# Experts' token rows kept in 32-bit floats, turned two blocks ahead, and a router stage with logits from 16-bit halves

## The chip, the cores and the metric

One core of one Trainium2 chip runs the whole program. The metric is device time in microseconds (us); the median of three runs of the kernel before is 1145.98 us (1141.5 to 1146.59).

## What is computed

Input x is 8 x 256 tokens of width 512, with a context of the same shape. Two layers follow each other: a long convolution used as attention, a quantised feed-forward net, a cross attention, and a mixture of experts. The change is in the last of them. Cut to what matters:

```
x2  = layernorm(x)                                   # 2048 tokens, D = 512
aff = sigmoid(x2 @ wa)                               # 16 experts
p, i = top_k(aff, 2);  p = p / sum(p)
expert(e, x2) = (gelu(x2 @ g[e] + gb[e]) * (x2 @ w1[e] + b1[e])) @ w2[e] + b2[e]     # F = 256
routed = sum over the 2 chosen experts of p * expert(e, x2)
shared = expert of sg[0] + expert of sg[1], on all tokens
out = x + shared + routed        # x2 also enters as the layer's own input in the kernel: x + x2
```

Products are made to nearly 32-bit precision from 16-bit (bf16) halves: a number is split into a high half and the rest, and three of the four products of halves are summed (`three_products`, L1138).

## The kernel before

Partitions hold 128 tokens; NT = 16 such tiles make the 2048 tokens. Every stage is one block with a program for each engine (SyncE issues most DMAs, VectorE is DVE, ScalarE is ACT, GpSimd is POOL, TensorE is PE). The engines' orders are written out by hand; they wait for each other by counted semaphores. A stage begins when all engines have left the one before.

**Attention** (`stage_attention`, from L1565 on) comes ahead of the router. In its last microseconds DVE makes the first two normalised tiles of the router (`RouterScales`, L1537, tiles r_xn).

**Router stage** (`stage_router`, L2029 to L2182, from 728 to 776 us). For each tile t of 16:

- DVE normalises a tile into xn, one of two buffers (L1561).
- ACT makes the high half of the token-major row (r_rows, L2167), DVE the low half (L2110), and SyncE stores both as 1024 bf16 numbers a token to token_rows in DRAM (L2076). This is what the experts later gather.
- PE transposes the tile (four 128x128 float transposes, L2143, into one of four PSUM buffers ps_rx). ACT copies it once as floats (r_xT, L2171) and once as bf16 high half (L2174, tile s_xT), DVE makes the low half (L2112). Tiles 0 to 11 of the turned halves are stored too (L2079).
- PE computes the logits from the float copy: four float matmuls with 16 columns (L2149), into ps_rl.
- ACT writes the scaled residual (L2178); for ten tiles SyncE stores it to mid_rows (L2082).
- The six weights of the two shared experts (512 KB each) are loaded by SyncE at the stage's start (L2071), their high halves made by POOL (L2095) and their low halves by DVE (L2116, `weight_lows`).

At the end ACT takes the exponential of all logits (L2180), DVE finishes the sigmoid (L2130, L2131), and the stage ends.

**Route and shared stage** (`stage_route_and_shared`, 776 to 885 us): top 2, the table of slots that sorts (token, expert) pairs into NBLK = 47 blocks of 128, the shared experts, and the loading and splitting of all routed experts' up and gate weights into the SBUF tensor expert_weights. At its end POOL gathers the rows of the first two blocks (L2375).

**Experts stage** (`stage_experts`, L2609 to L2954, from 885 us on). Block n of 47 goes through these steps:

- POOL gathers 128 rows from token_rows into e_rows (an indirect DMA of 256 KB, L2664), two blocks ahead. After it POOL issues the scatter of an older block's results (L2669), in the order gather(n + 2), scatter(n - 2).
- PE turns the rows: eight bf16 transposes (L2871), four of the high and four of the low halves, into ps_ex. The row's columns are taken with a step of four (`c:...:DC`), since the weights' partitions are laid out so. Here the transposed data is the stationary operand, loaded by LDWEIGHTS, and the identity is the moving one.
- ACT copies the high (L2736), DVE the low half (L2781) to e_xT.
- DVE copies the block's expert from expert_weights to e_w (L2774).
- PE makes gate and up (24 matmuls each, e_w stationary, e_xT moving, ps_eg and ps_eu), ACT the gelu (L2729), DVE the product with up (L2787), ACT and DVE its halves (L2742, L2795), PE the down product (six matmuls of 512 columns, ps_ed) with e_parts, which SyncE loads per block (512 KB, L2686), ACT scales it by the routing weight (e_yo, L2720).

PE's order is up(n), turn(n + 1), down(n - 1). On ACT it is out_rows(n - 2), gelu(n), x_split(n + 1), y_split(n); on DVE gate(n), x_split(n + 1), y_split(n), weights(n + 2). From block 32 on SyncE also loads the residual tiles (16 of 256 KB, L2694) while the blocks run.

After the last block come two chunks of the shared experts that were kept back (late_up, late_down), and the sums.

The bf16 view with a step of two (`a.bitcast(BF16)[:, :, :, 1::2]`, L1588), by which the upper 16 bits of floats serve as high halves with no copy, is already used in attention, for the stationary operand of the values' matmuls (L1865, tiles at_pf and kw).

Of the kernel before, what the change touches and what calls it, by code (L numbers as in the profile page):

```python
# [15 lines left out]
P = 128  # L16
# [1514 lines left out]

FRONT = 4
# [4 lines left out]
class RouterScales:  # L1537


    def __init__(self, sb, semaphore):  # L1540
        self.mean, self.var, self.tmp, self.rstd, self.gain, self.shift = (
            sb(f"r_{n}", [P, NT], F32) for n in ("mean", "var", "tmp", "rstd", "gain", "shift"))
        self.xn = [sb(f"r_xn{i}", [P, D], F32) for i in range(2)]
        self.var_ready, self.rstd_ready, self.scaled, self.xn_ready = (
            semaphore(f"rs_{n}") for n in ("var", "rstd", "sca", "xn"))

# [13 lines left out]
    def normalise(self, dve, x, t):  # L1560
        dve.tensor_scalar(self.xn[t % 2][:, :], x[:, t, :], self.mean[:, t:t + 1], self.rstd[:, t:t + 1], ALU.subtract, ALU.mult)\  # L1561
# [3 lines left out]
def stage_attention(k, ks, last_keys, v_hi, v_lo, qw, ow, vectors, x_mean, x_rstd, stats, qs, kb, ahead, front):  # L1565
# [3 lines left out]
    with ExitStack() as ctx:  # L1569
# [59 lines left out]
        def _(sp):  # L1629
# [364 lines left out]
SH_N = 2  # L1994
FE = 256
# [10 lines left out]
SETS = 4  # L2006
# [22 lines left out]
def stage_router(k, stats, xaff, sgu, sd, down_bias, kept, front, x_places):  # L2029
# [4 lines left out]
    with ExitStack() as ctx:  # L2034
# [4 lines left out]
        xT = two("r_xT", [P, DC, P], F32)  # L2039
        rows = [sb(f"r_rows{i}", [P, 2, D], BF16) for i in range(SETS)]  # L2040
# [5 lines left out]
        raw = [sb(f"r_raw{i}", [P, 1024], F32) for i in range(6)]  # L2046
        w_loaded, w_high = [k.semaphore(f"r_w{i}") for i in range(6)], k.semaphore("r_whi")
        rows_high, rows_low = k.semaphore("r_rh"), k.semaphore("r_rl")
# [3 lines left out]
        wa_loaded, dve_step, added, x_psum, xT_ready, x_high, x_low, logits, exped = (  # L2052
            sem(n) for n in ("wa", "dve", "add", "xp", "xT", "xh", "xl", "log", "ex"))
# [8 lines left out]
        def _(sp):  # L2062
# [6 lines left out]
            for n in range(6):  # L2069
                src = k.ins[("L1_ffn_sg", "L1_ffn_sw1")[dst[n][2]] if n < 4 else "L1_ffn_sw2"][dst[n][1], :, :]  # L2070
                sp.dma_start(raw[n][:, :].rearrange("p (c n) -> p c n", c=D // P if n < 4 else F2),  # L2071
                             src.rearrange("(c p) n -> p c n", p=P)).then_inc(w_loaded[n], 16)
            for t in range(NT):
                q = t % SETS
                sp.wait_ge(rows_low, t + 1)
                sp.dma_start(rows_dram[t, :, :], rows[q][:, :, :].rearrange("p s d -> p (s d)")).then_inc(rows_stored[q], 16)  # L2076
# [12 lines left out]
        def _(pool):  # L2089
            pool.memset(bias_raw[:, :], 0.0).then_inc(bias_zeroed, 1)  # L2090
            pool.wait_ge(front.var_ready, 2)
            front.inverse_root(k, pool, LAST)
            for n in range(6):
                pool.wait_ge(w_loaded[n], 16)
# [4 lines left out]
        def _(dve):  # L2099
            link = Link(dve, dve_step)  # L2100

            def normalise(t):
                dve.wait_ge(x_psum, t - 1)
                dve.wait_ge(rows_low, t - 1)
                front.normalise(dve, k.x, t)

            def split(t):
                q = t % SETS
                dve.wait_ge(rows_high, t + 1)
                dve.tensor_tensor(rows[q][:, 1, :], xn[t % 2][:, :], rows[q][:, 0, :], ALU.subtract).then_inc(rows_low, 1)  # L2110
# [6 lines left out]

            for t in range(NT):
# [8 lines left out]
                if t >= 5 and t % 2:  # L2127
                    weight_lows((t - 5) // 2)
# [8 lines left out]
        def _(pe):  # L2137
            def turn(t):
# [3 lines left out]
                for c in range(DC):  # L2142
                    last = pe.transpose(psX[t % SETS][:, c * P:(c + 1) * P], xn[t % 2][:, c * P:(c + 1) * P], k.ident[:, :])  # L2143
                last.then_inc(x_psum, 1)

            def score(t):
                pe.wait_ge(xT_ready, t + 1)
                for c in range(DC):
                    last = pe.matmul(psL[:, t * E_N:(t + 1) * E_N], xT[t % 2][:, c, :], wa[:, c, :], start=(c == 0), stop=(c == DC - 1))  # L2149
                last.then_inc(logits, 1)  # L2150

            pe.wait_ge(wa_loaded, 16)
            turn(0)
            turn(1)
            for t in range(NT):
# [5 lines left out]
        def _(act):  # L2161
            for t in range(NT):
                q = t % SETS
                act.wait_ge(xn_ready, t + 1)
                if t >= SETS:
# [909 lines left out]
```

## Time and profile before

| what | value |
|---|---|
| median of three runs | 1145.98 us |
| the profiled execution's own time | 1146.08 us |
| its span (first to last instruction) | 1144.3 us |
| PE busy | 1044.4 us (91%) |
| DVE, ACT, POOL busy | 830.1, 685.7, 582.5 us |
| bytes moved by DMA | 194.61 MB, 170 GB/s in the mean |
| router stage | 728 to 776 us |
| experts stage with its late part | 885 us to the end |

In the views below, times are us and "mean ns of one" is in nanoseconds. PEld is the weight load of TensorE, which overlaps its matmuls. PEclk is the granted clock of TensorE as a share of 2.4 GHz, so 0.5 is the lower level of 1.2 GHz. Matmuls overlap in the pipeline: the distance of two of them, not the length of one, is what a stream of them costs.

### The profile page before, as it was taken

Reading aid. Unit: us, or ns where it says so; the run is one execution under the profiler, and the core shown is the slowest. Engines: PE = TensorE matmul, PEld = TensorE weight load, DVE = VectorE, ACT = ScalarE, POOL = GpSimd, SP = SyncE. Lnnn points to the kernel's source line nnn. Section 1 sums busy time; section 2 is a strip of 40 time slices with the busy share of each in tenths; the row PEclk is TensorE's granted clock in tenths of the full one; section 3 lists DMA queues with packets and bytes.
Section 4 is the critical chain, followed back from the end, with each engine's and each line's share of the span. In section 5 each row is a group of like instructions: output and inputs, shape, how many; then the busy total and the mean of one; then the engine's idle time right before and its main releaser. Section 6 shows DMA issues by size and latency. Waiting matters only on the chain. (4 is left out here: it accounts for less than half of the span.)

```text
span 1144.3 us, 24806 instructions
## 1 busy us (share of the span) xinstructions
PE 1044.4 (91%) x9247; PEld 782.7 (68%) x9247; DVE 830.1 (73%) x1468; ACT 685.7 (60%) x1203; POOL 582.5 (51%) x635
## 2 busy tenths in 40 slices
PE   5999998679997998858999999798898899999997
PEld 5777776634443776547888876596675788888884
DVE  5589999869998788756666676698766555555538
ACT  4574773679986646557877775395354354445431
POOL 5444445425445354448777787403785355555520
PEclk9999999779999999959999999658999899999998
DMA  8483431859886223222222220484786467678879
GB/s 317 161 261 120 163 124 38 158 166 230 232 224 181 85 73 104 70 86 57 57 57 57 58 56 2 149 317 169 204 276 222 166 235 247 227 250 279 304 256 363
DMA packets 133705, 194.61 MB, mean 170 GB/s; under 512 B 67990, under 2 KB 70204, under 8 KB 132792
## 3 DMA queue, kind: packets, MB, share of 16 engines
q1 hardware_dynamic: 117256, 149.45, 41.9%
q0 software_dynamic: 8544, 24.68, 6.8%
q10 hardware_dynamic: 7792, 18.96, 5.1%
q8 instruction: 72, 1.18, 0.4%
q14 instruction: 41, 0.34, 0.1%
HBM read 127.47 MB, written 44.48 MB: 150 GB/s over the span
## 5 line engine op out<-in xcount | busy, mean ns | idle before, releaser
L470 PE MATMUL ps_y<-kv,toep 128*128 128x288 f32 x640 | 158.2, 410 | 3.4 <-PEq L173 2.2
L470 PEld LDWEIGHTS ps_y<-kv,toep 128*128 128x128 f32 x640 | 122.0, 192 | 39.0 <-DMA toep<-taps_padded 3.2
L1790 DVE TENSOR_REDUCE at_negmax<-ps_s 128x4 f32<-128x1024 f32 x64 | 78.2, 1222 | 49.2 <-PE ps_s L1840 49.2
L164 POOL TENSOR_TENSOR kv<-kx 128x1024 f32<-128x1024 f32 x32 | 60.6, 1895 | 86.3 <-DVE outT L524 37.6
L2669 POOL DMA_INDIRECT expert_results<-e_yo,target x47 | 68.9, 1467 | 57.9 <-ACT e_yo L2720 57.9
L1141 PEld LDWEIGHTS ps_eg<-e_xT,e_w 128*128 128x128 bf16 x1128 | 69.0, 100 | 15.2 <-DVE e_w L2774 2.5
L1141 PE MATMUL ps_eg<-e_xT,e_w 128*128 128x128 bf16 x1128 | 73.1, 223 | 4.1 <-DVE e_xT L2781 4.0
L1141 PE MATMUL ps_eu<-e_xT,e_w 128*128 128x128 bf16 x1128 | 72.0, 221 | 0.0
L2774 DVE COPY e_w<-expert_weights 128x4096 bf16 x47 | 57.7, 1227 | 18.3 <-issue 18.3
L2664 POOL DMA_INDIRECT e_rows<-token_rows,token x45 | 43.7, 970 | 50.9 <-PE ps_ex L2871 45.0
L2787 DVE SCALAR_TENSOR_TENSOR e_y<-ps_eu,e_bias,e_y 128x128 f32<-128x128 f32 x94 | 28.6, 346 | 55.4 <-PE ps_eu L1141 53.5
L1094 PE MATMUL ps_fH<-w1T,f_qaT 128*128 128x512 bf16 x256 | 64.2, 395 | 3.4 <-PEq L636 2.1
L1141 PEld LDWEIGHTS ps_eu<-e_xT,e_w 128*128 128x128 bf16 x1128 | 66.4, 99 | 0.0
L1110 PE MATMUL ps_fY<-w2T,f_qbT 128*128 128x512 bf16 x256 | 57.7, 379 | 5.7 <-DMA f_qbT<-f_qb 5.7
L2736 ACT ACTIVATE e_xT<-ps_ex 128x512 bf16<-128x512 bf16 x47 | 28.1, 597 | 57.8 <-PE ps_ex L2871 57.8
L1687 POOL TENSOR_TENSOR vw<-kw 128x1024 bf16<-128x1024 f32 x32 | 60.6, 1895 | 3.1 <-ACT kw L1743 3.1
L1687 POOL TENSOR_TENSOR vw<-at_pf 128x1024 bf16<-128x1024 f32 x32 | 60.6, 1895 | 0.0
L494 DVE TENSOR_TENSOR prod<-ps_y,qx 128x1024 f32<-128x1024 f32 x32 | 39.1, 1222 | 24.8 <-ACT ps_y L417 24.8
L1141 PE MATMUL ps_ed<-e_parts,e_yhi 128*128 128x512 bf16 x188 | 55.9, 379 | 0.7 <-DVE e_ylo L2795 0.4
L1749 ACT ACTIVATE qs<-ps_m 32x256 bf16<-32x256 bf16 x128 | 48.1, 376 | 11.5 <-PE ps_m L1852 8.4
L2729 ACT ACTIVATE e_y<-ps_eg,e_bias 128x128 f32<-128x128 f32 x94 | 29.4, 364 | 39.4 <-PE ps_eg L1141 26.0
L1094 PEld LDWEIGHTS ps_fH<-w1T,f_qaT 128*128 128x128 bf16 x256 | 25.4, 100 | 36.5 <-issue 5.7
(450 smaller groups left out, 3075.2 us busy)
## 6 DMA issues: line engine op xcount, KB each, us to landing
e_parts<-down_parts SPq DMA_DIRECT2D x47, 512.0 KB
w_raw<-in_L_ffn_w ACTq DMA_DIRECT2D x32, 512.0 KB, 4.2
toep<-taps_padded SPq DMA_DIRECT2D x32, 256.0 KB, 3.6
f_draw<-in_L_ffn_rw SPq DMA_DIRECT2D x16, 512.0 KB, 4.3
down_parts<-f_dparts SPq DMA_DIRECT2D x16, 512.0 KB, 2.9
expert_weights<-expert_results SPq DMA_DIRECT2D x16, 512.0 KB, 10.0
x_res<-in_x SPq DMA_DIRECT2D x4, 1024.0 KB
c_in<-in_ctx SPq DMA_DIRECT2D x4, 1024.0 KB, 14.3
```

What stands on the lines that cost most here:

```text
L164: pool.tensor_tensor(pairs[:, :, :, 0:HD0], x[:, :, 0:HD0].unsqueeze(2).broadcast_to([P, ROWS_N, WIDE, HD0]), sliding_rows(x, 0, 1, WIDE), ...
L470: last = pe.matmul(y[:, l * B:(l + 1) * B, :, WIDE - 1:], toep[h % 2][:, (DC - 1 - l + m) * P:(DC - l + m) * P], kv[h % 2][:, m * B:(m + 1 ...
L494: dve.tensor_tensor(slots[:, :, 0:WIDE, :], blocks(y)[:, :, :, WIDE - 1:PITCH - 1], sliding_rows(q, 0, 1, WIDE), ALU.mult) .then_inc(prod_ ...
L1094: pe.matmul(psH[:, f, :].rearrange("p (a t) -> p a t", t=P), qaT[p][:, c, :], k.w1T[:, f * DC:(f + 1) * DC, c, :], start=(c == 0), stop=False)
L1110: last = pe.matmul(psY[p][:, :].rearrange("p (a t) -> p a t", t=P), qbT[p][:, c, :], k.w2T[:, :, c, :], start=(c == 0), stop=(c == FC - 1))
L1141: instruction = pe.matmul(out, stationary[a], moving[b], start=first and n == 0, stop=last and n == 2)
L1687: pool.tensor_tensor(pl[u % 4][:, :, :, :], pf[u % 4], ph[u % 4], ALU.subtract)\
L1749: act.activation(qs[nb % 2][STACK:, h0 + j, c, :], psM[rows, :, :].rearrange("p q t -> p (q t)"), ACT.Copy)\
L1790: dve.tensor_reduce(negmax[u % 2][:, :].rearrange("p (j q) -> p j q", j=2), psS[:, :, :, :], AX.X, ALU.max, negate=True).then_inc(max_read, 1)
L2664: pool.indirect_dma_start(out=rows[j % 2], out_offset=None, in_=k.scratch["rows"], in_offset=bass.IndirectOffsetOnAxis(ap=token[:, j:j + 1 ...
L2669: pool.indirect_dma_start(out=k.scratch["results"], out_offset=bass.IndirectOffsetOnAxis(ap=target[:, j:j + 1], axis=0), in_=yo[j % 2], in ...
L2774: dve.tensor_copy(w1[j % 2][:, :, :, :].rearrange("p h c f -> p (h c f)"), W[:, bass.ds(e, 1), :, :, :].rearrange("p o h c f -> p (o h c f ...
```

## The change

Four parts, as the diff has them.

1. token_rows holds one float row (512 floats, 2048 bytes, as many as before) instead of two bf16 halves. The router stores xn itself; r_rows and its two operations a tile go away. xn gets four buffers instead of two.
2. In the experts stage PE turns the float rows with four float transposes in place of eight bf16 ones. ACT copies them as floats to e_xf, whose upper 16 bits, seen with a step of two, are the high half; DVE subtracts to make the low half e_xlo. The turn, ACT's and DVE's part come two blocks ahead (PE: up(n), turn(n + 2), down(n - 1)), with the order on DVE gate(n), y_split(n), x_split(n + 2), weights(n + 2), and two turns ahead of the loop.
3. The logits are computed by `three_products` on the turned halves and on the halves of wa (12 bf16 matmuls a tile); the float copy r_xT goes away, and score(t) waits for x_low instead.
4. Two of the six shared weights are loaded at the start of attention; the other four are loaded at tiles 1, 3, 5 and 7 of the router stage. `weight_lows` begin at tile 3, and POOL makes the first weight's high half ahead of the inverse root.

```diff
 class RouterScales:
-        self.xn = [sb(f"r_xn{i}", [P, D], F32) for i in range(2)]
+        self.xn = [sb(f"r_xn{i}", [P, D], F32) for i in range(SETS)]
+        self.raw = [sb(f"r_rawa{i}", [P, D // P * FE], F32) for i in range(RAW_AHEAD)]
+    def load_shared_weight(self, sp, k, n):
+        sp.dma_start(self.raw[n][:, :].rearrange("p (c n) -> p c n", c=D // P), self.shared_weight(k, n)).then_inc(self.raw_loaded[n], 16)
...
 stage_attention, sync:
+            for n in range(RAW_AHEAD):
+                front.load_shared_weight(sp, k, n)
             for b, u in STEPS:
...
 stage_router, sync:
-            for n in range(6):
-                src = ...
-                sp.dma_start(raw[n]..., src...).then_inc(w_loaded[n], 16)
             for t in range(NT):
-                sp.wait_ge(rows_low, t + 1)
-                sp.dma_start(rows_dram[t, :, :], rows[q][:, :, :]...).then_inc(rows_stored[q], 16)
+                if t % 2 and RAW_AHEAD + t // 2 < 6:
+                    sp.dma_start(raw[n]..., front.shared_weight(k, n)).then_inc(w_loaded[n], 16)
+                sp.wait_ge(xn_ready, t + 1)
+                sp.dma_start(rows_dram[t, :, :], xn[q][:, :]).then_inc(rows_stored[q], 16)
 vector:
             def normalise(t):
-                dve.wait_ge(x_psum, t - 1)
-                dve.wait_ge(rows_low, t - 1)
+                if t >= SETS:
+                    dve.wait_ge(x_psum, t - SETS + 1)
+                    dve.wait_ge(rows_stored[t % SETS], 16 * (t // SETS))
             def split(t):
-                dve.wait_ge(rows_high, t + 1)
-                dve.tensor_tensor(rows[q][:, 1, :], xn[t % 2][:, :], rows[q][:, 0, :], ALU.subtract).then_inc(rows_low, 1)
-                if t >= 5 and t % 2:
-                    weight_lows((t - 5) // 2)
+                if t >= 3 and t % 2 and t < 15:
+                    weight_lows((t - 3) // 2)
 tensor:
             def score(t):
-                pe.wait_ge(xT_ready, t + 1)
+                pe.wait_ge(x_low, t + 1)
                 for c in range(DC):
-                    last = pe.matmul(psL[...], xT[t % 2][:, c, :], wa[:, c, :], ...)
+                    last = three_products(pe, psL[...], [turned[t % SETS][:, s, c, :] for s in range(2)],
+                                          [wa_parts[:, s, c, :] for s in range(2)], c == 0, c == DC - 1)
 scalar:
-                act.activation(rows[q][:, 0, :], xn[t % 2][:, :], ACT.Copy).then_inc(rows_high, 1)
-                act.activation(xT[t % 2][:, :, :], chunks(psX[q][:, :]), ACT.Copy).then_inc(xT_ready, 1)
...
 stage_experts:
-        xT = two("e_xT", [P, 2, DC, P], BF16)
+        xf = two("e_xf", [P, DC, P], F32)
+        x_hi = [a.bitcast(BF16)[:, :, 1::2] for a in xf]
+        x_lo = two("e_xlo", [P, DC, P], BF16)
 scalar:
-                act.activation(xT[j % 2][:, 0, :, :], psX[0][:, :, :], ACT.Copy).then_inc(x_high, 1)
+                act.activation(xf[j % 2][:, :, :], psX[j % 2][:, :, :], ACT.Copy).then_inc(x_high, 1)
-                if n + 1 < NBLK:
-                    x_split(n + 1)
+                if n + 2 < NBLK:
+                    x_split(n + 2)
 vector:
-                dve.tensor_copy(xT[j % 2][:, 1, :, :], psX[1][:, :, :]).then_inc(x_low, 1)
+                dve.tensor_tensor(x_lo[j % 2][:, :, :], psX[j % 2][:, :, :], x_hi[j % 2], ALU.subtract).then_inc(x_low, 1)
 tensor:
             def turn(j):
                 pe.wait_ge(rows_loaded[j % 2], 16 * (j // 2 + 1))
-                for h in range(2):
-                    for c in range(DC):
-                        last = pe.transpose(psX[h][:, c, :], rows[j % 2][:, h * D + c:(h + 1) * D:DC], k.ident_b[:, :])
+                if j >= 2:
+                    pe.wait_ge(x_low, j - 1)
+                for c in range(DC):
+                    last = pe.transpose(psX[j % 2][:, c, :], rows[j % 2][:, c:D:DC], k.ident[:, :])
             for n in range(NBLK + 1):
-                if n + 1 < NBLK:
-                    turn(n + 1)
+                if n + 2 < NBLK:
+                    turn(n + 2)
```

## Rows read from the trace of the kernel before

**Rows 1.** Experts stage, windows: busy time (x count) of each engine, clock, DMA.

```profile
900.00:1045.00 145.00, 144.98 (x2031) 121.40 (x2028) 84.72 (x165) 72.61 (x163) 80.78 (x65) 1.00 0.69 238
1045.00:1094.00 49.00, 48.64 (x683) 40.72 (x681) 28.30 (x56) 23.80 (x55) 25.84 (x21) 1.00 0.89 307
```

**Rows 2.** The chain that ended last, one block: start, length, what.

```profile
1087.13 0.45 PE ps_ex L2871 x8
1087.58 1.29 PE ps_ed L1141 x6
...
1091.55 0.45 PE ps_ex L2871 x8
```

**Rows 3.** Router stage, window: its full stretch, columns as in Rows 1.

```profile
732.00:764.00 32.00, 30.80 (x147) 29.87 (x146) 28.80 (x52) 28.71 (x52) 8.07 (x7) 0.50 1.03 377
```

**Rows 4.** Router stage, timeline: start, length, engine, line, op.

```profile
756.08 1.09 PE L2143 MATMUL ps_rx<-ident,r_xn 128*128 128x128 f32 x4
756.97 1.73 PE L2149 MATMUL ps_rl<-r_wa,r_xT 128*128 128x16 f32 x8
758.54 1.09 PE L2143 MATMUL ps_rx<-ident,r_xn 128*128 128x128 f32 x4
...
772.71 0.38 ACT L2180 ACTIVATE r_exp<-ps_rl 128x256 f32<-128x256 f32 x1 [1.44 <-PE ps_rl L2149]
```

**Rows 5.** Start of the experts stage, PE alone, timeline.

```profile
896.39 2.72 PE L1141 MATMUL ps_eg<-e_xT,e_w 128*128 128x128 bf16 x24 [1.66 <-DVE e_xT L2781]
900.57 0.61 PE L2871 MATMUL ps_ex<-ident_b,e_rows 128*128 128x128 bf16 x8
```

**Rows 6.** Groups of DVE instructions by line, 728 to 773 us.

```profile
L2112 DVE TENSOR_TENSOR s_xT<-ps_rx,s_xT 128x512 bf16<-128x512 f32 x16 | 11.0, 684 | 5.1 <-ACT s_xT L2174 5.1
L1561 DVE TENSOR_SCALAR r_xn<-x_res,r_mean,r_rstd 128x512 f32<-128x512 f32 x14 | 7.9, 565 | 0.0
L2116 DVE TENSOR_TENSOR sgu<-r_raw,sgu 128x1024 bf16<-128x1024 f32 x4 | 4.9, 1217 | 0.0
```

**Rows 7.** Attention, a run of float transposes of adjacent columns, timeline.

```profile
606.74 1.07 PE L1929 MATMUL ps_p<-ident,at_o 128*128 128x128 f32 x8
```

**Rows 8.** Float transposes of every second column (8 bytes apart), timeline.

```profile
872.18 0.44 PE L2588 MATMUL ps_stab<-ident,s_table 47*128 47x47 f32 x2
```

**Rows 9.** Float transposes and weight loads by tile: ns min/median/max of one, first and last start.

```profile
L1929 PE MATMUL ps_p<-ident,at_o x64: 272/273/474, 550.7 to 718.0; 128*128 128x128 f32 x64
L1929 PEld LDWEIGHTS ps_p<-ident,at_o x64: 138/141/230, 550.7 to 717.8; 128*128 128x128 f32 x64
L2588 PE MATMUL ps_stab<-ident,s_table x2: 292/304/317, 872.2 to 872.3; 47*128 47x47 f32 x2
L2588 PEld LDWEIGHTS ps_stab<-ident,s_table x2: 194/205/216, 872.2 to 872.3; 47*128 47x128 f32 x2
L1865 PEld LDWEIGHTS ps_o<-v_hi,at_pf x256: 96/97/151, 506.4 to 712.2; 128*128 128x128 bf16 x128
L2871 PEld LDWEIGHTS ps_ex<-ident_b,e_rows x376: 111/113/131, 885.1 to 1096.1; 128*128 128x128 bf16 x188
```

**Rows 10.** Experts stage, one block on POOL, timeline.

```profile
965.38 1.50 POOL L2669 DMA_INDIRECT expert_results<-e_yo,target  x1 [1.05 <-ACT e_yo L2720]
966.89 0.61 PE L2871 MATMUL ps_ex<-ident_b,e_rows 128*128 128x128 bf16 x8
967.77 0.97 POOL L2664 DMA_INDIRECT e_rows<-token_rows,token  x1 [0.90 <-PE ps_ex L2871]
```

**Rows 11.** Early experts stage: a gather's issue, and windows in which it lands.

```profile
891.14 0.97 POOL L2664 DMA_INDIRECT e_rows<-token_rows,token  x1 [5.90 <-issue]
...
892.00:894.00 2.00, 2.00 (x22) 1.90 (x19) 0.00 (x0) 0.00 (x0) 0.11 (x1) 0.81 0.47 135
```

**Rows 12.** A scatter of the loaded stretch, and ACT waiting for it.

```profile
1058.41 1.55 POOL L2669 DMA_INDIRECT expert_results<-e_yo,target  x1 [1.05 <-ACT e_yo L2720]
...
1067.50 0.69 ACT L2720 ACTIVATE e_yo<-ps_ed,weight 128x512 f32<-128x512 f32 x1 [1.61 <-DMA expert_results<-e_yo,target]
```

More of the change, by code:

```diff
@@ L1993 @@
 E_N = 16
-SH_N = 2
-FE = 256
 F2 = FE // P
@@ L2038, in stage_router @@
         gain, shift, xn, scaled, xn_ready = front.gain, front.shift, front.xn, front.scaled, front.xn_ready
-        xT = two("r_xT", [P, DC, P], F32)
-        rows = [sb(f"r_rows{i}", [P, 2, D], BF16) for i in range(SETS)]
+        wa_parts = sb("r_wap", [P, 2, DC, E_N], BF16)
         turned = [kept[q // ST][:, q % ST, :, :].rearrange("p s (c t) -> p s c t", c=DC) for q in range(SETS)]
@@ L2142, in turn @@
                 for c in range(DC):
-                    last = pe.transpose(psX[t % SETS][:, c * P:(c + 1) * P], xn[t % 2][:, c * P:(c + 1) * P], k.ident[:, :])
+                    last = pe.transpose(psX[t % SETS][:, c * P:(c + 1) * P], xn[t % SETS][:, c * P:(c + 1) * P], k.ident[:, :])
                 last.then_inc(x_psum, 1)
             def score(t):
-                pe.wait_ge(xT_ready, t + 1)
+                pe.wait_ge(x_low, t + 1)
                 for c in range(DC):
-                    last = pe.matmul(psL[:, t * E_N:(t + 1) * E_N], xT[t % 2][:, c, :], wa[:, c, :], start=(c == 0), stop=(c == DC - 1))
+                    last = three_products(pe, psL[:, t * E_N:(t + 1) * E_N], [turned[t % SETS][:, s, c, :] for s in range(2)],
+                                          [wa_parts[:, s, c, :] for s in range(2)], c == 0, c == DC - 1)
                 last.then_inc(logits, 1)
-            pe.wait_ge(wa_loaded, 16)
             turn(0)
             turn(1)
+            pe.wait_ge(wa_low, 1)
             for t in range(NT):
@@ L2624, in stage_experts @@
         bias = sb("e_bias", [P, 2 * F2, NBLK], F32)
-        psX = [ctx.enter_context(nc.psum_tensor(f"ps_ex{i}", [P, DC, P], BF16)) for i in range(2)]
+        psX = [ctx.enter_context(nc.psum_tensor(f"ps_ex{i}", [P, DC, P], F32)) for i in range(2)]
         late_psG, late_psU = ([ctx.enter_context(nc.psum_tensor(f"ps_e{n}{i}", [P, F2, CHUNK], F32)) for i in range(2)] for n in "gu")
@@ L2906, in _ @@
             turn(0)
+            turn(1)
             for n in range(NBLK + 1):
@@ L3013, in build @@
             late_xT = left(moe, "s_xT0", [P, ST, 2, DC * P], BF16)
-            e_rows = [a[:, :] for a in (left(moe, f"e_rows{i}", [P, 2 * D], BF16) for i in range(2))]
+            e_rows = [a[:, :] for a in (left(moe, f"e_rows{i}", [P, D], F32) for i in range(2))]
             e_yo = [a[:, :] for a in (left(moe, f"e_yo{i}", [P, D], F32) for i in range(2))]
```

65 lines of the change are left out of this document (35 added, 30 removed).

## The prediction

> **What bounds the kernel now.** I read the windows first, since the share of busy time over the whole program mixes stages. In the experts stage PE is busy for 144.98 of 145 us at the full clock, and for 48.64 of 49 in the stretch with the residual loads; DVE, ACT and POOL have more than a third of their time free [rows 1]. The chain of waits, read next, runs there through PE alone: from one block's transposes to the next it takes 1091.55 - 1087.13 = 4.42 us, of which the eight transposes are 0.45, the down product 1.29, gate and up the rest [rows 2]. So in this stage whatever PE is given or spared counts 47 times, and work on ACT and DVE counts only if it comes late.
>
> The router stage is less plain. In the 32 us from 732 on PE, DVE and ACT are each busy for 29 to 31, and the DMA engines are full too (share 1.03, 377 GB/s) [rows 3]. The timeline shows who sets the pace: PE goes from transposes (1.09) to the float logits (1.73) and on with no gap, one tile each 758.54 - 756.08 = 2.46 us, at the lower clock (0.50, that is 1.2 GHz, though PE never rests), and the exponential at 772.71 waits for PE [rows 3, 4]. DMA is the second limit, close behind: the bytes of the last four tiles are few, so only PE is late at the end.
>
> **The change, part by part.** *Router.* PE's 1.73 a tile become 12 bf16 matmuls of 16 columns. No row shows one. From above they cost what bf16 matmuls of 128 columns take at the lower clock, 2.72 / 24 = 0.11 each [rows 5], 1.3 us a tile; from below almost nothing. I take 0.7, nearer the bottom since 16 columns are few. With 0.9 for the transposes (four in 1.09, their pipeline's tail overlapped) PE needs 1.6 a tile, at most 2.2. DVE loses its subtraction for the rows and keeps 0.68 for the turned half, 0.57 for xn and 6 x 1.22 / 16 = 0.46 for weights [rows 6], 1.7 a tile. ACT keeps two of its four operations. The three hand over to each other (score now waits for DVE's low half), and tile t + 2 is turned while t is split; I allow 1.85 a tile.
>
> DMA: 32 us at 377 GB/s are 12.06 MB [rows 3]. Behind 764 only four stores of rows are left, 1.05 MB in all. Two weights of 524 kB move into attention, where DMA has room, so 12.06 + 1.05 - 1.05 = 12.1 MB stay; 1.05 of them are the rows of the last four tiles, which don't hold anyone up. 11.0 MB at 377 GB/s take 29 us from 732, to 761. The engines at 1.85 a tile from 731 come to 760.6. Both limits meet, and the last logits follow at about 763 instead of 772.7 [rows 4]: -9.5 us. What follows (exponential, reciprocal, start of the next stage) is unchanged. Bounds: with PE at 2.2 a tile 766.5 or -6; with DVE alone at 1.7 and DMA at 400 GB/s 759.5 or -13. The two loads in attention and the third and fourth xn buffer cost nothing: no engine waits on them. Cover gone would mean the first weight's high half late, which POOL has idle time for.
>
> *Start of the experts stage.* Today up(1) waits until 896.39 for DVE's copy, which stands behind the bias work, though PE had turned its rows by 896.39 - 1.66 = 894.73; the idle 1.66 us leave PE at the lower clock again, and gate and up of this block last until 900.57, 4.18 us instead of 4.42 - 0.45 - 1.29 = 2.68 [rows 2, 5]. After the change block 1 is turned and split ahead of that, so up(1) follows the turn at once. The first split on DVE is a subtraction (as long as the one of 0.68 [rows 6]) instead of a copy; I allow 0.25 for it. Then 894.73 + 0.25 + 2.68 = 897.7, against 900.57: -2.9. If the clock stays low, -1.2.
>
> *Turns.* Eight bf16 transposes in 0.45 [rows 2] become four float ones. Float transposes of adjacent columns stand (1.07 - 0.27) / 7 = 0.114 apart [rows 7, 9], so four take 0.46. But here the columns are 16 bytes apart. The nearest row has them 8 bytes apart: two in 0.44, one of 0.30, so 0.14 apart, with loads of 205 ns instead of 141 [rows 8, 9]. I take 0.123 (between the two, as the load of one hides behind the matmul of the other): 0.49 a block, +0.04, x 47 = +2 us. From below 0.114: +0.3 us. From above: see the first rival.
>
> The Trainium skill speaks against this very step: "Advanced Engine Details and Errata", section Memory Cachelines, has 16-byte lines in SBUF, of which at least two hits are needed to hide the access, and a penalty where each access meets another line. At 8 bytes there are two hits a line, and by the rule no loss; the rows show one already. At 16 bytes there is one hit. By that rule the sum gets the first rival's price.
>
> The high half as moving operand with a step of 4 bytes has no row. As stationary operand the same view loads in 97 ns, against 113 for bf16 with 8 bytes [rows 9], so I put it at 0; from above, if it halved the rate of the 32 matmuls of a block that read it, 32 x 2.68 / 48 = 1.8 us a block [rows 2].
>
> ACT's float copy and DVE's subtraction (at most 0.68 more a block on an engine with 1.8 us of each 4.42 free [rows 1, 6]) are hidden, since the order on both engines now makes them a block early.
>
> *The gather.* This is where two blocks in advance costs. POOL issues gather(n + 3) behind scatter(n - 2). The gather was held by the turn at 966.89 and issued at 967.77 [rows 10], for a turn two periods on, 975.7: 7.0 us behind the issue's end at 968.74. Now its buffer is free a block earlier, but the scatter ahead of it still waits for ACT: it ends at 966.88, the gather at 967.9, and its turn is due at 966.89 + 4.42 = 971.3. The slack falls from 7.0 to 3.4 us. In the quiet stretch that is enough: a gather whose issue ended at 892.11 had moved its 0.26 MB by 894.0, 1.9 us (135 GB/s over 2 us) [rows 11]. In the loaded stretch (share 0.89 [rows 1]) a scatter whose issue ended at 1059.96 still held ACT at 1067.50, 7.5 us on [rows 12]. That is the extreme, with the gather's own landing in a full queue below it. When a gather is late by d, a loop of two blocks lengthens by d, so a block by d / 2, and slower blocks load the queues less. For the 11 blocks from 1045 to 1094 I take d = 0.5: +3 us; bounds 0 and +12 (d = 2.2).
>
> *Sum:* -9.5 - 2.9 + 2 + 3 = -7.4. The profiled execution took 1146.08 us (span 1144.3 and 1.8 around it), 0.1 over the median of 1145.98; so I forecast 1138.6 us.
>
> **Rivals.** *1. Weight loads 16 bytes apart pace PE (slower).* The mechanism: a float transpose waits for its own LDWEIGHTS, and at this step that outlasts the matmul. For it: 4 bytes to 8 costs a float load 64 ns (141 to 205), 4 to 8 in bf16 16 ns (97 to 113) [rows 9]; if each further 4 bytes cost a float load the same, 16 bytes give 141 + 3 x 64 = 333 ns, 192 more, of which the 8-byte row hid about 40: 0.114 + 0.15 = 0.26 apart. If instead the rate only halves once more, 0.20. I take 0.23: four take 0.92, +0.47 x 47 = +22 us. PE slower gives the gathers time, so their +3 goes. Net -12.4 + 22 = +9.6: 1155.6. Against it: a load may have a floor that 8 bytes already meet. It decides from where the distance exceeds 0.114 + 9.4 / (47 x 4) = 0.164; below that the kernel stays faster.
>
> *2. Gathers late throughout the loaded stretch.* With d = 2.2 the 3 us become 12: 1147.6, no change. For it the 7.5 us of [rows 12]; against it, gather and scatter now follow each other instead of crossing the e_parts loads.
>
> *3. The router stays with DMA.* If the stores' waits (four buffers, SyncE's fixed order) hold its pace and only 4 of the 9.5 us come: 1144.1. For it the share of 1.03 [rows 3].
>
> *4. The moving operand's step halves PE's rate:* -7 + 47 x 1.8 = +78 us, 1224. Against it the stationary row.
>
> **How the numbers follow.** Forecast 0.50, rival 1 0.30, rival 2 0.12, rival 3 0.05, rival 4 0.03. Likeliest: 1138.6, its own range 1132 to 1144 (router -13 to -6, gathers 0 to +5, turns 0.3 to 5). The whole range goes down to 1132 and up to 1160, so that rival 1 at 0.26 apart is just in (+28 for the turns, 1162, is a little over). About 0.5% (5.7 us) is what a measurement tells from no change. Faster: 0.8 of the forecast, a little of rivals 2 and 3, 0.44. Slower: nine tenths of rival 1, half of rival 2, rival 4: 0.36. The rest, 0.20, is the same.
>
> **What would show it.** Right: ps_ex transposes about 0.12 apart and a block of 4.46 us in the chain; no gap before up(1); r_exp at about 763; PE idle before ps_ex on DMA e_rows only behind 1045, some 5 us in all. Rival 1: ps_ex 0.2 or more apart, LDWEIGHTS of ps_ex near 300 ns, blocks of 4.8 us or more. Rival 2: PE idle on e_rows over 10 us. Rival 3: DVE or ACT waiting for token_rows or turned_tiles stores, r_exp at 768. Rival 4: ps_eg matmuls 0.08 apart or more. The forecast is wrong if blocks exceed 4.6 us.

## The result, and the profile after

| | time, median | runs |
|---|---|---|
| changed kernel | 1159.01 us | 4, 1157.91 to 1166.29 |
| kernel before, same chip | 1146.28 us | 4, 1141.5 to 1152.5 |

The ratio is 1.0116, with a 95% interval of 1.009 to 1.0143: the change costs 1.2%, where 1138.6 us was forecast. The profiled execution took 1159.22 us with a span of 1157.5, 13.2 more than the span before. The windows of the changed kernel come first (columns as in [rows 1] and [rows 3]).

```profile
732.00:764.00 32.00, 19.38 (x208) 15.29 (x208) 22.60 (x36) 16.85 (x27) 5.86 (x6) 0.50 1.01 356
900.00:1045.00 145.00, 139.81 (x1750) 118.24 (x1779) 84.92 (x153) 67.38 (x153) 82.73 (x62) 1.00 0.71 228
1045.00:1094.00 49.00, 42.04 (x513) 35.04 (x520) 24.62 (x44) 19.71 (x45) 22.18 (x18) 0.97 0.73 250
```

The router's row shows PE's part of the forecast: it is busy for 19.38 of 32 us where it was 30.80. In the experts stage PE was busy for 144.98 of 145 us; now 5.2 us are missing in the quiet stretch and 7.0 of 49 in the loaded one. The tile view of e_rows in the changed kernel says what they wait for (ns min/median/max of one, first and last start; the last row is idle time ahead of all instructions that touch the tile, us and times).

```profile
L2883 PEld LDWEIGHTS ps_ex<-ident,e_rows x188: 195/212/226, 880.1 to 1104.3; 128*128 128x128 f32 x188
L2883 PE MATMUL ps_ex<-ident,e_rows x188: 283/285/488, 880.2 to 1104.4; 128*128 128x128 f32 x188
...
  DMA e_rows<-token_rows,token: 24.6, 25
```

24.6 us counts both of PE's queues, weight loads and matmuls, and so cannot be added to the span as it stands. Most of it falls behind 1036, where SyncE begins to load the residual tiles. The same row for the windows 895:1036 and 1036:1110:

```profile
  DMA e_rows<-token_rows,token: 6.5, 12
  DMA e_rows<-token_rows,token: 17.3, 11
```

The distances from one turn's start to the next say what this costs. Without a wait they are 4.57 us. Up to 1036 seven of them are longer by 0.1 to 0.9 us each; with 0.05 for the block behind each, 4.2 us are lost there. Of the 12 blocks from 1036 on seven are longer by 0.1 to 3.7 us, 10.7 us in all. The longest wait also slows what follows (timeline):

```profile
1071.78 1.13 PE L2883 MATMUL ps_ex<-ident,e_rows 128*128 128x128 f32 x4 [3.51 <-DMA e_rows<-token_rows,token]
```

After 3.51 us of idleness the granted clock was 0.83 in the mean of 1070 to 1080, where it was 1.00 before and after. The turn took 1.13 us and the five down matmuls behind it 2.06, where 0.75 and 1.24 are usual behind a wait. This one event cost 5.1 of the 10.7 us. The chain of waits of the changed kernel shows how one late gather of the quiet stretch holds everything (start, length, what):

```profile
940.00 0.54 PE ps_ex L2883 x4
940.54 0.05 issue
940.59 1.26 PE ps_ed L1141 x5
941.85 0.03 issue
941.87 0.70 ACT e_yo L2733
942.57 0.27 issue
942.84 1.69 POOL expert_results L2682
944.52 0.30 issue
944.83 4.66 DMA e_rows<-token_rows,token
949.49 0.04 issue
949.53 0.75 PE ps_ex L2883 x4
```

Read it as a loop. The turn at 940.00 is followed by the down product of an earlier block, ACT scales the result (e_yo), POOL's scatter of 1.69 takes it away, 0.30 later POOL issues the next gather, and its rows let the turn of 949.53 start. The DMA piece of 4.66 includes the issue of 0.97 itself, so the rows landed 3.69 us behind the issue's end. Without the wait this turn would have come two blocks of 4.57 us behind 940.00, at 949.14. It came at 949.53, and four transposes behind a wait take 0.75 us and not 0.54.

The router of the changed kernel, by the tile views of r_xn and r_exp:

```profile
L1575 DVE TENSOR_SCALAR r_xn<-x_res,r_mean,r_rstd x16: 531/539/1352, 720.1 to 762.1; 128x512 f32<-128x512 f32 x16
...
  DMA token_rows<-r_xn: 8.5, 5
```
```profile
L2191 ACT ACTIVATE r_exp<-ps_rl x1: 384/384/384, 765.8 to 765.8; 128x256 f32<-128x256 f32 x1
```

The first normalise stands at 720.1 (722.5 before) and r_exp at 765.8 (772.71 before [rows 4]). So 2.4 of the 6.9 us were there before the stage began; the first normalise of the profiles of this study lies anywhere between 718.8 and 725.9 us. The stage itself went from 50.2 to 45.7 us. DVE now waits for stores of token_rows, 8.5 us in all.

Where the 13.2 us of span come from, all read as stretches between two instructions of the two traces:

| stretch | before | after | difference |
|---|---|---|---|
| up to the first r_xn | 722.5 | 720.1 | -2.4 |
| router, to r_exp | 50.2 | 45.7 | -4.5 |
| from there to the first ps_ex | 112.4 | 114.3 | +1.9 |
| to the end of up(1) | 15.5 | 12.8 | -2.7 |
| the other blocks | 203.0 | 223.8 | +20.8 |
| late part | | | +0.1 |

The +1.9 goes with a lower granted clock in the shared expert's stage (0.95 in the mean of it, 0.97 before) and was not followed up.

### The profile page after: what moved, and what is told of

It is laid out like the page before. It is cut to its first block and busy times, and to the rows that moved or that the text cites. A ratio compares the mean times of both kernels' runs of the same rounds, so it can differ in the third digit from the quotient of the medians.

```text
span 1157.5 us, 24323 instructions
## 1 busy us (share of the span) xinstructions
PE 1026.3 (89%) x9044; PEld 763.5 (66%) x9123; DVE 831.8 (72%) x1453; ACT 670.7 (58%) x1172; POOL 589.7 (51%) x635
## 5 line engine op out<-in xcount | busy, mean ns | idle before, releaser
L2682 POOL DMA_INDIRECT expert_results<-e_yo,target x47 | 76.6, 1630 | 97.5 <-ACT e_yo L2733 97.5
L1141 PE MATMUL ps_eg<-e_xf,e_w 128*128 128x128 bf16 x752 | 73.1, 221 | 1.3 <-DVE e_xlo L2794 1.3
L2750 ACT ACTIVATE e_xf<-ps_ex 128x512 f32<-128x512 f32 x47 | 28.1, 597 | 76.8 <-PE ps_ex L2883 65.5
L1141 PE MATMUL ps_eu<-e_xf,e_w 128*128 128x128 bf16 x752 | 72.4, 219 | 0.0
L1141 PE MATMUL ps_eg<-e_xlo,e_w 128*128 128x128 bf16 x376 | 67.5, 219 | 0.0
L1141 PE MATMUL ps_eu<-e_xlo,e_w 128*128 128x128 bf16 x376 | 66.9, 218 | 0.0
L1141 PEld LDWEIGHTS ps_eg<-e_xf,e_w 128*128 128x128 bf16 x752 | 59.5, 97 | 7.1 <-DVE e_w L2789 1.7
L1141 PEld LDWEIGHTS ps_eu<-e_xf,e_w 128*128 128x128 bf16 x752 | 59.1, 96 | 0.0
L2808 DVE TENSOR_TENSOR e_ylo<-e_y,e_yhi 128x256 bf16<-128x256 f32 x47 | 20.0, 425 | 49.2 <-ACT e_yhi L2756 37.3
L1765 ACT ACTIVATE qs<-ps_m 32x256 bf16<-32x256 bf16 x128 | 48.1, 376 | 11.6 <-PE ps_m L1868 8.4
```

The source lines that it names most:

```text
L1141: instruction = pe.matmul(out, stationary[a], moving[b], start=first and n == 0, stop=last and n == 2)
L1765: act.activation(qs[nb % 2][STACK:, h0 + j, c, :], psM[rows, :, :].rearrange("p q t -> p (q t)"), ACT.Copy)\
L2682: pool.indirect_dma_start(out=k.scratch["results"], out_offset=bass.IndirectOffsetOnAxis(ap=target[:, j:j + 1], axis=0), in_=yo[j % 2], in ...
```

## The experiments

The theory behind all of them: the gather is issued behind the scatter and so comes too late for a turn two blocks in advance. Rivals: the gathers are late because the queues are loaded at any order; the step of 16 bytes or the moving operand's step costs the time.

**Gather first.** Only POOL's order is changed:

```diff
+            gather(2)
             for n in range(NBLK + 2):
-                if n + 2 < NBLK:
-                    gather(n + 2)
+                if n + 3 < NBLK:
+                    gather(n + 3)
                 if n >= 2:
                     scatter(n - 2)
```

> The changed kernel with one thing moved: on POOL the gather of block n+3 is issued ahead of the scatter of block n-2 (the gather of block 2 right after those of 0 and 1), where the changed kernel issues gather(n+2) right behind... the scatter of the block before. Theory A (the 24.6 us that PE waits for e_rows come from the gather being queued behind POOL's scatter, so that it is issued too late for a turn two blocks ahead): the waits on e_rows fall from 24.6 us (both of PE's queues) to under 4, the experts stage loses about 13 us, span about 1145, time about 1146. Theory B (the gathers are late because the DMA queues are loaded, or because the scattered rows' packets go ahead of the gathered ones at whatever time the gather is issued): the waits stay above 15 us and the time stays within 3 us of 1159. If A holds and the rest of the block is as in the changed kernel, the block takes 4.57 us all through the quiet stretch against 4.42 before.

Measured: 1145.57 us (10 runs), ratio 0.9999 (0.9975 to 1.0022). 13.4 us are back, as theory A has it. In its tile view of e_rows no wait for the gather's DMA is left. What gathers wait for now is the turn, as they should, since the turn frees their buffer:

```profile
  PE ps_ex L2884: 39.6, 43
```

Its chain has blocks of 959.97 - 955.40 = 4.57 us and nothing but PE:

```profile
955.40 1.37 PE ps_eg L1141 x24
956.76 1.37 PE ps_eu L1141 x24
958.13 0.54 PE ps_ex L2884 x4
...
958.72 1.24 PE ps_ed L1141 x5
959.97 1.08 PE ps_eg L1141 x19
```

The landing of each gather can be read from the completions of its 16 DMA engines; in the kernels with (nearly) all of them recorded, counted from the end of the issue:

```
us behind the issue's end      905-1040 (min/median/max)   1045-1094
gather first                   2.4 / 2.9 / 4.4             4.7 / 5.95 / 6.2
changed, down weights cut      2.2 / 2.4 / 3.7             2.4 / 3.4 / 3.65
```

(The second row is a run that comes further down.)

The changed kernel leaves 949.14 - 945.80 = 3.3 us for this, the kernel before and this one about 7. The landing is not shorter with the gather first, it is covered. In the quiet stretch the median of 2.9 would fit into 3.3 as well and only the slowest gathers would be late; in the loaded stretch none of these would fit.

**One block in advance.** The changed kernel with turn and x_split one block ahead, in the orders of the kernel before:

```diff
-                if n + 2 < NBLK:
-                    turn(n + 2)
+                if n + 1 < NBLK:
+                    turn(n + 1)
```

and the same for ACT's and DVE's x_split, which on DVE again stands ahead of y_split.

> The changed kernel with the rows turned and split one block ahead again, in the order of the kernel before, everything else as changed (rows in float, split after the turn). Theory A (late gathers, because the turn two blocks ahead takes one block's time out of the slack): waits on e_rows under 2 us, blocks of 4.57 us, the start of the experts stage 1 to 3 us later than in the changed kernel: about 1146 to 1150. Theory B (gathers late by the load of the queues): waits stay above 15 us, 1158 to 1162. Theory C (turning one block ahead leaves the turn's product on the path ahead of the gate matmuls, since ACT and DVE split it only then): PE waits for e_xf or e_xlo in each block, 0.3 us or more a block, 1160 or more.

Measured: 1161.73 us, ratio 1.0133 (1.0095 to 1.0171). The waits on the gather are gone here too (none in the tile view), yet the kernel is no faster. Its chain:

```profile
999.39 1.24 PE ps_ed L1141 x5
1000.63 0.17 issue
1000.79 1.53 PE ps_eg L1141 x24
1002.32 1.37 PE ps_eu L1141 x24
1003.69 0.54 PE ps_ex L2881 x4
```

and the timeline of the same block has the split that the gate waits for:

```profile
1000.00 0.69 DVE L2793 TENSOR_TENSOR e_xlo<-ps_ex,e_xf 128x512 bf16<-128x512 f32 x1 [0.34 <-ACT e_xf L2750]
```

Before each gate PE stands for 0.17 us until DVE has written e_xlo, and the gate takes 1.53 us instead of 1.37, since the first matmul after a stop costs its full 0.22 us and not the distance of 0.057 to the next. A block takes 4.89 us, 0.32 more than with the gather first; over 47 blocks 15 us, against 16.2 measured between the two. Theory C was right, and the forecast of 1146 to 1150 for A was a miss: a subtraction that starts only when ACT has finished its copy does not fit into the down product's 1.24 us. Turning two blocks in advance is what the float rows need; only the gather must not pay for it.

**The high half dense.**

```diff
-        xf = two("e_xf", [P, DC, P], F32)
-        x_hi = [a.bitcast(BF16)[:, :, 1::2] for a in xf]
+        x_hi = two("e_xhi", [P, DC, P], BF16)
```

ACT's copy then writes x_hi, and DVE's subtraction and PE read it.

> The changed kernel with the high half written by ACT as a dense 16-bit tile, where the changed kernel reads every second 16-bit element of the float tile as the moving operand. Theory A (the every-second-element read costs PE 1.37 against 1.34 us for the 24 matmuls of a gate or an up): gate and up go back to 1.34, PE works 0.06 us less a block, 2.8 us over 47 blocks; as PE waits for gathers in every second block or so, between 0 and 3 us of that reach the end: 1156 to 1159. Rival (the 0.03 belongs to something else, such as more traffic on the tiles while PE reads): gate and up stay at 1.37 and the time stays within 1 us of 1159. ACT's write may take longer or shorter by a few ns: no effect.

Measured: 1161.65 us (4 runs, 1152.69 to 1165.53), ratio 1.0116 (1.0054 to 1.0179), not to be told from the changed kernel, and above the 1156 to 1159 that theory A gave. The chain in a stretch without a wait has gate and up at 1.34:

```profile
1025.48 1.34 PE ps_eg L1141 x24
1026.82 1.34 PE ps_eu L1141 x24
```

but the waits for gathers grew from 24.6 us to

```profile
  DMA e_rows<-token_rows,token: 30.6, 26
```

So the first half of theory A is shown: the step of the moving operand costs 0.03 us in 24 matmuls. That the saved time goes into waiting, because the loop over POOL and the DMA sets the pace, fits the longer waits; the run with all three edits tests it.

**Adjacent columns.** The rows are permuted when they are normalised, so that the turn loads adjacent float columns:

```diff
-        dve.tensor_scalar(self.xn[t % SETS][:, :], x[:, t, :], ...
+        dve.tensor_scalar(self.xn[t % SETS][:, :].rearrange("p (c q) -> p c q", c=D // P),
+                          x[:, t, :].rearrange("p (q c) -> p c q", c=D // P), ...
...
-                    last = pe.transpose(psX[j % 2][:, c, :], rows[j % 2][:, c:D:DC], k.ident[:, :])
+                    last = pe.transpose(psX[j % 2][:, c, :], rows[j % 2][:, c * P:(c + 1) * P], k.ident[:, :])
```

with the router's and the shared expert's gate and up weights loaded in the matching order.

> The changed kernel with the columns of the rows permuted when they are normalised (the vector engine reads the rows of x in steps of 4 elements and writes a token row with the columns c, c+4, c+8 ... adjacent), so that the turn of an expert's rows loads adjacent float columns where the changed kernel loads them in steps of 16 bytes; the weights of the router and of the shared expert are laid out to match. Theory A (the step costs, as the 205 ns weight loads at 8-byte steps against 141 ns at adjacent ones say): the four turns of a block are 0.12 apart or less against 0.14, a turn falls from about 0.59 to 0.47, PE works 0.12 us less a block, 5 us over 47 blocks, of which the waits for gathers may eat part: 1153 to 1158. Rival (the turn's pace is that of its float moving pass, at any step): turns stay at 0.14, time within 1 us of 1159. The normalising operation on DVE in the router stage may be slower by its step: if it goes from 0.57 to over 0.9 us each, DVE becomes the end of that stage and up to 5 us come back.

Measured: 1156.8 us, ratio 1.0102 (1.0071 to 1.0133), inside the range expected, though not separate from the changed kernel by its interval. The profiled execution was the fastest of the six (1151.08 us, the slowest 1161.36), so its waits are likely at the low end. Tile view and chain:

```profile
L2884 PEld LDWEIGHTS ps_ex<-ident,e_rows x188: 137/140/143, 877.7 to 1096.3; 128*128 128x128 f32 x188
...
  DMA e_rows<-token_rows,token: 21.9, 32
```

```profile
950.19 1.37 PE ps_eu L1141 x24
951.55 0.44 PE ps_ex L2884 x4
```

The weight load falls from 212 to 140 ns and a turn from 0.54 to 0.44 us. Of 47 x 0.10 = 4.7 us the medians show 2.2, which is less than can be told apart here. DVE's normalise takes 744 ns instead of 539, and the router does not notice (stage 46.9 us).

**All three together.**

> The changed kernel with the three edits of the earlier runs together: gather ahead of scatter on POOL, the high half written dense by ACT, the columns permuted at the normalise so that the turn loads adjacent columns. Theory A (three separate causes, which add): no waits on e_rows; the chain's block is 0.44 for the turn, 1.29 or 1.30 for down with its hand-over, 2 x 1.34 for gate and up, 4.42 in all as before the change (4.57 with the gather alone moved); then over 46 blocks 6.5 us less than with the gather alone: span about 1137.5, time about 1139, some 6 us or 0.6% under the kernel before, which is the router's and the experts' start's share. Rival (with every block back at the pace of before, the gather of the loaded stretch is late again, or the dense high half brings nothing while the matmuls wait for their weights): block 4.46 or more, or waits on e_rows of over 4 us: 1142 or more.

Measured: 1137.61 us (7 runs), against 1144.49 for the kernel before on that chip; ratio 0.9942 (0.9921 to 0.9963). This is faster than both kernels. One block of its chain:

```profile
1001.83 1.34 PE ps_eg L1141 x24
1003.17 1.34 PE ps_eu L1141 x24
1004.51 0.44 PE ps_ex L2884 x4
...
1005.01 1.24 PE ps_ed L1141 x5
1006.25 1.34 PE ps_eg L1141 x24
```

1006.25 - 1001.83 = 4.42 us, the pace of [rows 2] to the hundredth. No gather is waited for, so theory A holds and the causes add: a block takes 0.15 us less than with the gather alone moved (0.10 from the turn, 2 x 0.03 from gate and up).

**The same order in the kernel before.**

```diff
-                if n + 2 < NBLK:
-                    gather(n + 2)
                 if n >= 2:
                     scatter(n - 2)
+                if n + 2 < NBLK:
+                    gather(n + 2)
```

> The kernel BEFORE the change, with one thing moved on POOL: scatter(n-2) is issued ahead of gather(n+2), where the kernel before issues the gather first. Nothing is turned in advance. Theory A (the order gather behind scatter costs, whichever kernel it is in, once the slack is too small): the gather now waits for ACT's e_yo and stands behind a 1.5 to 1.7 us scatter, so its end is about 4 us later and the slack falls from 7.0 to about 3; PE waits for e_rows in many blocks, 8 to 25 us in all, and the time is 1153 to 1165. Theory B (the late gathers need the turn two blocks in advance, with its loop over the buffer): no waits on e_rows, within 2 us of 1146.5.

Measured: 1163.05 us, ratio 1.0169 (1.0129 to 1.021). In its tile view of e_rows:

```profile
  DMA e_rows<-token_rows,token: 25.4, 30
```

Turned one block in advance, in 16-bit rows, with nothing else of the change: the same 25 us of waiting, and about 19 us lost. It is the order and the slack, not the float rows; theory A's range of 1153 to 1165 holds.

**Down weights cut.** The changed kernel, order and all, but a block's down weights are not fetched in full:

```diff
+                w = 2 * F2 * D if j < 2 else 2 * P
-                sp.dma_start(parts[j % 2], expert_down_parts(k)[bass.ds(e, 1), :, :]...
+                sp.dma_start(parts[j % 2][:, 0:w], expert_down_parts(k)[bass.ds(e, 1), :, 0:w]...
```

> The changed kernel, in which from block 2 on only the first 256 of the 4096 16-bit columns of a block's down weights are loaded (32 of 512 KB per partition set; the down products then use what is left of an earlier expert's, so this part of the result is left wrong). POOL's order and its work stay. It asks whether a gather issued behind the scatter is late by the order alone, or only because its rows then cross the 0.52 MB of down weights. Theory A (both: the order leaves 3.3 us from the end of the issue to the turn, an undisturbed gather lands in about 2, and the crossing makes it 2.4 to 3.7): the waits on e_rows fall from 24.6 to under 4 us, time 1144 to 1149. Rival B (the order alone is enough; the rows' own 512-element pieces and the scatter's writes ahead of them in the same queue fill the 3.3 us): the waits stay above 15 us, time 1155 or more.

Measured: 1146.41 us, ratio 1.003 (1.0 to 1.0061). Tile view and window:

```profile
  DMA e_rows<-token_rows,token: 3.1, 10
```

```profile
900.00:1045.00 145.00, 142.72 (x1808) 121.53 (x1837) 87.44 (x157) 69.74 (x158) 84.15 (x63) 1.00 0.42 134
```

With the DMA share at 0.42 instead of 0.71 the rows land in 2.4 us (median, table above), inside the 3.3. Theory A holds: it takes both, an order that leaves 3.3 us and 0.52 MB of other loads crossing in each block. Whether it matters that these are the down weights, or would be the same with any 0.52 MB, was not tested.

**Float logits again.** Built on the kernel with the gather first: ACT writes the turned tile in float too, and PE multiplies it in float as before.

```diff
-                    last = three_products(pe, psL[...], [turned[t % SETS][:, s, c, :] for s in range(2)], ...
+                    last = pe.matmul(psL[...], xT[t % 2][:, c, :], wa[:, c, :], start=(c == 0), stop=(c == DC - 1))
```

> The changed kernel with the gather first, and the router's logits from the float halves again (ACT writes the turned tile in float, and PE multiplies in float as in the kernel before); rows in float, four buffers and the two early weights stay. It is compared with the kernel that has the gather alone moved (1145.6, where the router stage took 47.5 us from the first normalise to r_exp; five kernels with the changed router took 44.8 to 47.5, the kernel before 50.2). Theory A (the logits are what the router gained by): the stage is at 49 to 51 us and the time 2 to 5 us above, 1148 to 1150. Theory B (the gain is by the bytes moved into attention and the fewer operations on DVE and ACT, and PE is not the limit): the stage stays at 45 to 48 us, the time within 2 us of 1145.6.

Measured: 1146.01 us, ratio 1.0018 (0.9999 to 1.0037). The stage takes 49.9 us from the first normalise to r_exp, as theory A has it, and PE has no gap in it:

```profile
740.00:764.00 24.00, 23.91 (x118) 23.80 (x117) 16.64 (x28) 17.07 (x29) 3.13 (x3) 0.50 1.03 379
```

Seven kernels with the changed router took 44.8 to 47.8 us, 46.4 in the mean, so the halves are worth 3.5 us of the stage, from single traces that lie 3.0 us apart among themselves. In the time it is 0.4 us of the medians and 0.2% of the ratios, less than can be told apart: the stage's part is shown, the gain at the end is not, and theory A's 1148 to 1150 was missed.

**More stores.** One line is added to the changed kernel's router stage, a second store of each of ten tiles of x:

```diff
+                    sp.dma_start(k.scratch["results"][2 * TOK + t * P:2 * TOK + (t + 1) * P, :], k.x[:, t, :]).then_inc(x_stored, 16)
```

> The changed kernel with each store of mid_rows in the router stage doubled (the second copy goes to rows of the results' memory that are not read): some 2.6 MB more to move in the stage, and no work more for PE, DVE or ACT. Theory A (the changed router is bound by DMA): at 377 GB/s the stage gets 6 to 7 us longer, r_exp moves by that and the time is about 1165. Theory B (the engines' hand-overs set its pace, DMA is hidden beside them): under 2 us more, about 1160.

Measured: 1170.57 us, ratio 1.0208 (1.0163 to 1.0253). Tile views of r_xn and r_exp:

```profile
L1575 DVE TENSOR_SCALAR r_xn<-x_res,r_mean,r_rstd x16: 531/546/1353, 724.4 to 772.0; 128x512 f32<-128x512 f32 x16
...
  DMA token_rows<-r_xn: 13.8, 9
```
```profile
L2192 ACT ACTIVATE r_exp<-ps_rl x1: 384/384/384, 775.6 to 775.6; 128x256 f32<-128x256 f32 x1
```

The stage is 775.6 - 724.4 = 51.2 us long, 4.8 more than the mean, for 2.6 MB; DVE's waits for stores grew from 8.5 to 13.8 us. That is theory A's side, though 1 to 2 us under its price of 6 to 7, so some of the bytes went into gaps. With the float logits PE paces the stage; with the halves it is the DMA for the most part. The time rose by 11.6 us, more than the stage explains. Of the 15.4 us between the two profiled executions 4.3 lie ahead of the first normalise, 5.5 in the stage, and 5.0 in the experts' blocks, where the gathers were later still; this edit touches neither the first nor the last, and why they differ stays open.

**The two early weights loaded late.** On the kernel with the gather first, the loads stand at the head of the router stage again:

```diff
-            for n in range(RAW_AHEAD):
-                front.load_shared_weight(sp, k, n)
             for b, u in STEPS:
...
 stage_router, sync:
+            for n in range(RAW_AHEAD):
+                front.load_shared_weight(sp, k, n)
             for t in range(NT):
```

> The changed kernel with the gather first, and the two weights that the changed kernel loads in the attention stage loaded at the head of the router stage again (1.05 MB). To compare with the kernel that has the gather alone moved (1145.6; stage of 47.5 us from the first normalise to r_exp, other kernels with this router 44.8 to 46.9). Theory A (the router is bound by DMA, as the 5.0 us for 2.6 MB more say): 1.05 MB at 377 GB/s are 2.8 us, stage 48 to 50 us, time 1147 to 1149. Rival (the bytes fit in the gaps at the head of the stage, where the DMA share is low): no change, 1145 to 1146.

Measured: 1144.96 us, ratio 1.001 (0.9988 to 1.0031); stage 48.1 us. The stage is 0.3 us longer than the longest of the seven, inside theory A's 48 to 50, but the time is unchanged, as the rival has it: the early loads of part four are worth nothing that can be measured at the end. In the 8 us from 732 on the DMA share is 0.97 here and 0.76 with the early loads, so most of the bytes fill a gap.

## Why the prediction was wrong

The step that failed is the gather's, the term of +3. The prediction did see that POOL's order takes the slack from 7.0 to 3.4 us, and the runs show 3.3. What it had wrong is how late the gathers then are: 0.5 us in the 11 blocks of the loaded stretch, and never in the quiet one. The term was 13.4 us (gather first against the changed kernel) and not 3, and both of its parts were short:

- In the loaded stretch the turns of the changed kernel lose 10.7 us. With the gather first a gather takes 4.7 to 6.2 us to land there, so against 3.3 us of slack it is late by 1.4 to 2.9 us and not by 0.5. The prediction had the 7.5 us of [rows 12] in hand and set it aside as the extreme. Rival 2, which was given 0.12, puts d at 2.2 and 12 us on this stretch: the size is about right, though near half of the 10.7 is the one long wait with the fall of the clock behind it.
- In the quiet stretch they lose 4.2 us, where the prediction had nothing. It called 3.4 enough, because one gather seemed to have landed in 1.9 us at 135 GB/s [rows 11]. By its completions that gather landed 2.3 us behind its issue's end, and it had the DMA engines nearly to itself. In the stretch at issue a block moves 1.05 MB, and a gather took 2.4 to 4.4 us. The stretch's own share of 0.69 stood in [rows 1]; the landing should have been read from the same stretch.

The other steps, with what they measured:

- Router, -9.5 forecast: -4.5. PE's part was right (12 logits' matmuls take 0.5 us), but of the two limits that met at 761 in the prediction the DMA's was set too low: the engines moved 356 GB/s in the 32 us from 732 and not 377, and stayed full until 764. And the four buffers tie DVE to the stores: the prediction put them at nothing, since no engine would wait on them, and DVE waited 8.5 us. Rival 3, which was given 1 in 20, is what the stage did, at nearly its price of 4.
- Start of the experts stage, -2.9 forecast: -2.7. The chain of the changed kernel has up(1) behind the turn of block 2 at once and at full clock (the turn itself waited 0.36 us for its gather, which the forecast did not have):

```profile
889.37 0.75 PE ps_ex L2883 x4
890.11 1.37 PE ps_eg L1141 x24
891.48 1.37 PE ps_eu L1141 x24
```

- Turns, +2 forecast at 0.49 a block: 0.54, +4.2 us.
- Moving operand, 0 forecast: 2 x 0.03 us a block, +2.7 us. The row of a stationary operand did not carry over to a moving one, though the step of 4 bytes costs far less than the bound of 1.8 a block.
- Rival 1 is out, though the time moved its way. Loads at 16 bytes take 212 ns, against 205 at 8 bytes and 141 adjacent [rows 9]; no turn comes near the 0.164 apart from which it decides. The rule of the Trainium skill that it cited ("Advanced Engine Details and Errata", Memory Cachelines) gives no loss at 8 bytes, with two hits a line, and one at 16. The traces show the loss at 8 and almost none on top at 16; the row at 8 bytes is two loads of a smaller tile (47 partitions), so the first of these two steps rests on little.
- Rival 2 was right for its stretch, as said above. Its 1147.6 is too low since it kept the -9.5 of the router and had nothing for the quiet stretch, little for the turns and nothing for the moving operand.
- Rival 4 is out: gate and up take 1.37 us each, not 1.34 + 0.9.

Together: -4.5 - 2.7 + 4.2 + 2.7 + 13.4 = +13.1. The -2.4 ahead of the router and the +1.9 behind it belong to no step.

## What to carry to other kernels

When work is moved ahead in time, list the transfers that feed it and ask which queue their issue stands in: here the operand was needed a block earlier, but the gather still stood behind a scatter that waits for the end of the block two before. A transfer's landing time is to be read in the stretch where it will run, with its usual neighbours; the same 0.26 MB took 2.3 us nearly alone, up to 4.4 beside the down weights and up to 6.2 beside the residual tiles too. And a loop that is closed over a wait can swallow what other edits save: two edits of the turn and of the moving operand, made one at a time, brought nothing that could be told from the changed kernel, and 0.57% together once the gather was moved.

## What was not expected of the hardware

- A float weight load's time goes 141, 205, 212 ns for columns 4, 8 and 16 bytes apart (the 205 from two loads of a smaller tile): nearly all of the loss is in the first step. From 4 to 16 bytes four transposes lose 0.10 us.
- A 16-bit moving operand read at every second element costs 1.37 us for the 24 matmuls of a gate, of which 16 read it, instead of 1.34.
- POOL's scatter of the same 0.26 MB took 1.69 us in the changed kernel and 1.50 before [rows 10], and 1.50 again in the kernel that turns one block in advance. The traces tie this to DVE's copy of the expert's weights, here in the changed kernel (its scatter is the one of 942.84 above) and in the kernel before (its scatter is the one of 965.38):

```profile
942.46 1.22 DVE L2789 COPY e_w<-expert_weights 128x4096 bf16 x1
964.80 1.23 DVE L2774 COPY e_w<-expert_weights 128x4096 bf16 x1 [0.33 <-issue]
```

The scatters end at 944.53 and 966.88, both 0.85 us behind the copy's end. The same holds for all 42 to 44 scatters of a kernel that start under a copy, in five traces, within 0.02 us; the three or four with no copy beside them take 0.96 to 0.98. In the changed kernel the copy starts only 0.38 us ahead of the scatter and not 0.57, so more of it is still to come. No run moved the copy alone.
